# Softmax attention: the low parts of the third expert weight on GpSimd in two operations

## The chip, the cores and the metric

The kernel runs on one core of a Trainium2 chip. The metric is the time of one execution on the device in microseconds (us), as the median of several executions; lower is better. The engines are TensorE (PE), VectorE (DVE), ScalarE (ACT), GpSimd (POOL) and SyncE (SP, which only issues DMAs here). Each runs its own queue of instructions in order, and they wait for each other by semaphores.

## What is computed

A decoder of two layers over x of 32 samples x 128 positions x 256 features: softmax attention, retention over a context, a mixture of eight experts, then three further stages. This case lies in the first stage. Its arithmetic per sample, with n the layer norm of x:

```
q = softmax(n Wq + bq, over the 256 features)
k = softmax(n Wk + bk, over the 128 positions)
v = softmax(n Wv + bv, over the 128 positions)
x = x + q (k^T v) / sqrt(256)
```

Beside it the first stage prepares data of later stages: the three expert weights W1, W2, W3 (each 128 x 8192 f32 in the kernel's layout) are multiplied by 256 and split into a high part in f16 and a low part in f16 (the value minus the high part), and both go to DRAM, where the expert stage reads them. The context is split in the same way, without a factor.

## The kernel before

The stage (softmax_attention) works in eight groups g of four samples (GB = 4, NG = 8). Each engine has one loop over j that takes, in an order written out by hand, steps of group j (projection of v and k), group j + 1 (statistics and normalisation) and group j - 1 (q, the product, the addition). PSUM is four areas pA to pD. I call a pass from one L483 to the next a round.

The weights' pieces: each weight w = 0, 1, 2 is cut into eight pieces n of 128x1024, one for each round, in two buffers each. SP loads piece n into pf[w][n % 2] (L347); ScalarE writes the high part to ph (L639, piece j in its pass j); VectorE writes the low part to pl by one scalar_tensor_tensor, pf x 256 - ph (L540, piece j - 1 in its pass j); SP waits for piece_low[w], stores both parts (L353) and loads piece n + 2, for w = 0, 1, 2 in turn.

VectorE's order in a pass: the addition to X (L534), statistics of the next group (L82 to L97), the shift of k (L496, L499), the reciprocal of v's sum (L504), the low part of the rows (L483), the largest of q (L514) and its shift (L516), the sum of k (L508, L510), the maximum of v (L489) and its shift (L496, L499), the low part of weight 1 (L540), qT (L523), the low parts of weights 0 and 2 (L540), the normalisation of the next group (L478), the reciprocal of q's sum (L527), the maximum of k (L489). In pass 3 centre_v follows (L546, L548), in passes 4 to 8 the low part of a retention weight (L554). The shifts L496 and L499 read and write 128x8 tiles in SBUF, L516 a 128x4 tile.

GpSimd's order in a pass: the reciprocal root of the next group's variance (invert, L675), the normalisation of v's exponentials (norm_v, L681), the low part of the context (context_lower, L686), both for group j - 1.

TensorE's order: the turned rows (L393), q (L419, L421), v (L262), the turned v (L430), the turned q (L438, which waits for ScalarE's exponentials L618, which wait for L516), k (L262), the product of k and q (attend, L445, which waits for qT), and the weighing of v (weigh, L453, which waits for ScalarE's copy L631). VectorE's addition L534 waits for L453.

Of the kernel before, what the change touches and what calls it, by code (L numbers as in the profile page):

```python
# [9 lines left out]
ALU = mybir.AluOpType  # L10
# [42 lines left out]
def spread(ap, n):  # L53

    return ap.unsqueeze(2).broadcast_to((ap.shape[0], ap.shape[1], n))
# [219 lines left out]
def softmax_attention(nc, sems, X, ident, power, A, ahead):  # L275

    SCALE = 16.0
    HALVES_SCALE = 256.0
    FEATURES = DC * GB
    with ExitStack() as scope:  # L280
        c = Core(nc, scope, sems, "a_")
# [23 lines left out]
        def samples(ps):  # L305
            return ps[:, :, :].rearrange("p a (b t) -> p (a b) t", t=S)
# [10 lines left out]
        def on(g, *work):  # L317
            if 0 <= g < NG:
                for w in work:
                    w(g)  # L320
# [3 lines left out]
        pf = [[c.sb(f"pf{w}{i}", [P, WIDE]) for i in range(2)] for w in range(3)]  # L324
        ph, pl = ([[c.sb(f"{n}{w}{i}", [P, WIDE], f16) for i in range(2)] for w in range(3)] for n in ("ph", "pl"))
        piece_in, piece_out = ([[c.sem(f"{n}{w}{i}") for i in range(2)] for w in range(3)] for n in ("piece_in", "piece_out"))
        piece_high, piece_low = ([c.sem(f"{n}{w}") for w in range(3)] for n in ("piece_high", "piece_low"))

        cf, ctx16 = ([c.sb(f"ctx{i}", [P, DC * GT]) for i in range(2)],
                     [[c.sb(f"ctx16{t}{i}", [P, DC * GT], f16) for i in range(2)] for t in range(2)])  # L330
# [7 lines left out]
        with nc.Block() as block:  # L338
# [128 lines left out]
            def _(dve):  # L467
# [18 lines left out]
                def maximum(n, ps):  # L486
                    def work(g):
                        dve.wait_ge(s[n + "_projected"], g + 1)
                        dve.tensor_reduce(mx[n][:, :], samples(ps), AX, ALU.max).then_inc(s[n + "max"], 1)  # L489
                    return work  # L490

                def shift(n, at):
                    def work(g):
                        bias = spread(bkv[:, at, :], GB)
                        dve.wait_ge(s[n + "max"], g + 1)
                        dve.scalar_tensor_tensor(by_chunk(mb[n]), by_chunk(mx[n]), 1.0 / SCALE, bias, ALU.mult, ALU.add)\  # L496
                           .then_inc(s[n + "maxb"], 1)
                        dve.wait_ge(s[n + "maxb"], g + 1)
                        dve.tensor_tensor(by_chunk(nb[n]), bias, by_chunk(mb[n]), ALU.subtract).then_inc(s[n + "shift"], 1)  # L499
                    return work  # L500
# [36 lines left out]
                def piece_lower(w):  # L537
                    def work(n):
                        dve.wait_ge(piece_high[w], n + 1)
                        dve.scalar_tensor_tensor(pl[w][n % 2][:, :], pf[w][n % 2][:, :], HALVES_SCALE, ph[w][n % 2][:, :],  # L540
                                                 ALU.mult, ALU.subtract).then_inc(piece_low[w], 1)
                    return work

                def centre_v():
                    dve.wait_ge(later_in, 16 * len(RETENTION))
                    dve.tensor_reduce(wsum[:, :], by_head, AX, ALU.add).then_inc(v_summed, 1)  # L546
                    dve.wait_ge(v_summed, 1)
                    dve.scalar_tensor_tensor(by_head, spread(wsum[:, :], HD), -1.0 / HD, by_head, ALU.mult, ALU.add)\  # L548
                       .then_inc(v_centred, 1)

                def later_lower(i):
                    n = RETENTION[i]
                    dve.wait_ge(later_high, i + 1)
                    dve.scalar_tensor_tensor(flat(R[n][1]), later[n], HALVES_SCALE, flat(R[n][0]), ALU.mult, ALU.subtract)\  # L554
                       .then_inc(later_low, 1)
# [14 lines left out]
                for j in range(NG + 2):  # L570
                    on(j - 2, add)
                    on(j + 1, stats)
                    on(j - 1, shift("k", 0))
                    on(j + 1, lambda g: rs.combine(dve, g))
                    on(j - 1, invert_v)
                    on(j, rows_low)
                    on(j - 1, shift_q, invert_k)
                    on(j, maximum("v", pD), shift("v", 1))
                    on(j - 1, piece_lower(1), take_q, piece_lower(0), piece_lower(2))
                    on(j + 1, norm)  # L580
                    on(j - 1, invert_q)
                    on(j, maximum("k", pC))
                    if j == 3:
                        centre_v()
                    if 0 <= j - 4 < len(RETENTION):
                        later_lower(j - 4)
# [84 lines left out]
            @block.gpsimd  # L671
            def _(pool):
                def invert(g):
                    pool.wait_ge(rs.ve_done, g + 1)
                    pool.tensor_tensor(rstd[:, :], rs.ve[:, :], power[:, 0:GB], ALU.pow).then_inc(s["rstd"], 1)  # L675

                def norm_v(g):
                    pool.wait_ge(s["vrec"], g + 1)
                    if g > 0:
                        pool.wait_ge(s["vn_turned"], g)  # L680
                    pool.tensor_tensor(samples(vn), samples(ex["v"]), spread(rec["v"][:, :], S), ALU.mult)\  # L681
                        .then_inc(s["vn"], 1)

                def context_lower(g):
                    pool.wait_ge(ctx_high, g + 1)
                    pool.tensor_tensor(ctx16[1][g % 2][:, :], cf[g % 2][:, :], ctx16[0][g % 2][:, :], ALU.subtract)\  # L686
                        .then_inc(ctx_low, 1)

                invert(0)
                for j in range(NG + 1):  # L690
                    on(j + 1, invert)
                    on(j - 1, norm_v, context_lower)


def starts(value, n):
# [2857 lines left out]
def decoder(nc, A, out, stages):  # L3553
    with ExitStack() as whole:
        c = Core(nc, whole, [], "")
        X = c.sb("X", [P, B, D])
        ident = c.sb("ident", [P, P])
        power = c.sb("power", [P, 64])
        work = {"softmax_attention": softmax_attention, "retention": retention, "moe_swiglu": moe_swiglu,
                "lie": lie_rotation, "mqa": one_key_attention, "moe_silu": moe_silu}  # L3560
        sems = []
# [124 lines left out]
```

## Time and profile before

| | us |
|---|---|
| median of 3 runs | 1486.89 |
| lowest and highest | 1485.07, 1488.93 |
| the profiled execution | 1483.58 |
| its span in the trace | 1481.8 |

The span is the time from the first to the last instruction in the trace; 1.8 us of the profiled execution lie around it. Times in the rows are counted from the start of the span. "Busy" is the time in which an engine has an instruction in work. Of TensorE the profile also gives the granted clock, as a share of 2.4 GHz: 1.00 or 0.50. The first stage takes the first 172 us of the span.

### The profile page before, as it was taken

To read this page: it belongs to the slowest core of one execution; us is meant where nothing else is said; L and a number is where in the kernel's file an instruction comes from. 1 tells how busy PE (TensorE), PEld (TensorE's weight loads), DVE (VectorE), ACT (ScalarE), POOL (GpSimd) and SP (SyncE) were. 2 spreads that over 40 slices of the span, in tenths; PEclk is the share of its full clock that TensorE was granted. 3 is DMA by queue.
4 is the path that set the end of the run, shared out by engine and by line. 5 is a ranking of instruction groups with operands and counts; after the bars stand their busy time and mean duration, and the time that the engine had idled before them with its cause. 6 is when DMAs were issued, how large, how long until landed. Compare 5 with 4: busy or idle time off the path is not lost. (4 is left out here: it accounts for less than half of the span.)

```text
span 1481.8 us, 29874 instructions
## 1 busy us (share of the span) xinstructions
PE 1209.2 (82%) x10673; PEld 871.6 (59%) x10673; DVE 1007.5 (68%) x2053; ACT 723.0 (49%) x1388; POOL 462.4 (31%) x437
## 2 busy tenths in 40 slices
PE   4999579989766379999999914992799976999997
PEld 2656356777545369999999902931445532665564
DVE  5999567887665846666666557575778785667653
ACT  4778455555324134444444414043356656756643
POOL 1322164564322044545455311156344211000000
PEclk9999789999996589999999965555899997999999
DMA  7666358567603722222332163001745403033131
GB/s 283 228 243 230 134 97 154 102 125 104 80 2 149 309 81 92 94 94 93 97 101 82 49 240 138 2 1 39 178 68 101 86 3 115 15 129 131 28 129 29
DMA packets 99977, 165.03 MB, mean 111 GB/s; under 512 B 14902, under 2 KB 63738, under 8 KB 98556
## 3 DMA queue, kind: packets, MB, share of 16 engines
q1 hardware_dynamic: 91964, 142.40, 34.2%
q0 software_dynamic: 7488, 20.46, 4.5%
q8 instruction: 92, 1.51, 0.4%
q14 instruction: 49, 0.40, 0.1%
q10 hardware_dynamic: 384, 0.26, 0.1%
HBM read 110.61 MB, written 52.30 MB: 110 GB/s over the span
## 5 line engine op out<-in xcount | busy, mean ns | idle before, releaser
L1075 POOL DMA_INDIRECT expert_results<-mt_yout,m_deliver x78 | 77.2, 990 | 149.2 <-ACT mt_yout L1163 137.2
L1108 PE MATMUL mt_pU<-mt_xh,m_w 128*128 128x256 f16 x624 | 116.2, 274 | 1.5 <-DVE mt_xl L1193 1.5
L1534 DVE TENSOR_TENSOR r_sim<-r_pS,r_causal 128x512 f32<-128x512 f32 x128 | 86.5, 683 | 43.8 <-PE r_pS L1444 43.0
L1108 PE MATMUL mt_pV<-mt_xh,m_w 128*128 128x256 f16 x624 | 115.4, 273 | 0.0
L1067 POOL DMA_INDIRECT mt_xin<-token_rows,m_fetch x78 | 86.7, 1111 | 81.4 <-POOLq L782 57.9
L2958 ACT ACTIVATE q_ex<-q_pE 128x512 f32<-128x512 f32 x128 | 75.1, 601 | 74.1 <-PE q_pE L2590 73.4
L1119 PE MATMUL mt_pY<-m_w,mt_hh 128*128 x624 | 106.4, 273 | 1.0 <-DVE mt_hl L1207 1.0
L1157 ACT ACTIVATE mt_hh<-ahead 128x512 f16<-128x512 f32 x78 | 49.2, 631 | 118.7 <-DVE ahead L1202 118.7
L3262 PE MATMUL s_pY<-s_w,s_hh 128*128 128x256 f16 x576 | 99.9, 273 | 8.0 <-DVE s_hl L3482 6.3
L2687 DVE TENSOR_REDUCE q_mx<-q_pS 128x4 f32<-128x512 f32 x128 | 85.4, 684 | 29.7 <-PE q_pS L2569 29.2
L1199 DVE TENSOR_TENSOR ahead<-mt_pU,ahead 128x512 f32<-128x512 f32 x78 | 54.0, 692 | 57.7 <-ACT ahead L1151 57.7
L1207 DVE TENSOR_TENSOR mt_hl<-ahead,mt_hh 128x512 f16<-128x512 f32 x78 | 54.0, 692 | 54.3 <-ACT mt_hh L1157 54.3
L3334 ACT ACTIVATE s_h<-s_pU,s_b 128x512 f32<-128x512 f32 x72 | 49.4, 687 | 81.5 <-PE s_pU L3248 81.3
L3475 DVE TENSOR_TENSOR s_hc<-s_h,s_spread_share 128x512 f32<-128x512 f32 x64 | 44.2, 691 | 65.2 <-ACT s_h L3334 65.2
L1108 PE MATMUL mt_pU<-mt_xl,m_w 128*128 128x256 f16 x312 | 85.6, 274 | 0.0
L1108 PE MATMUL mt_pV<-mt_xl,m_w 128*128 128x256 f16 x312 | 85.2, 273 | 0.0
L1119 PE MATMUL mt_pY<-m_w,mt_hl 128*128 x312 | 85.0, 273 | 0.0
L1151 ACT ACTIVATE ahead<-mt_pU 128x512 f32<-128x512 f32 x78 | 46.6, 597 | 65.8 <-PE mt_pU L1108 65.8
L3262 PE MATMUL s_pY<-s_w,s_hl 128*128 128x256 f16 x288 | 78.5, 273 | 0.0
L3248 PE MATMUL s_pU<-s_XH,s_w 128*128 128x512 f16 x216 | 73.1, 379 | 0.0
L3262 PEld LDWEIGHTS s_pY<-s_w,s_hh 128*128 128x128 f16 x576 | 52.3, 98 | 31.7 <-DVE s_hl L3482 15.0
L1108 PEld LDWEIGHTS mt_pU<-mt_xh,m_w 128*128 x624 | 61.4, 98 | 8.9 <-issue 1.9
(593 smaller groups left out, 3458.7 us busy)
## 6 DMA issues: line engine op xcount, KB each, us to landing
s_spread_share<-shares SPq DMA_DIRECT2D x32, 512.0 KB, 6.1
a_pf<-in_L_ffn_W SPq DMA_DIRECT2D x24, 512.0 KB, 6.4
m_w<-split_w SPq DMA_DIRECT2D x6, 2048.0 KB, 19.0
split_w<-a_ph SPq DMA_DIRECT2D x24, 256.0 KB, 3.8
split_w<-a_pl SPq DMA_DIRECT2D x24, 256.0 KB, 4.2
r_kstack<-k_bounce SPq DMA_DIRECT2D x48, 128.0 KB, 3.9
r_qstack<-q_bounce SPq DMA_DIRECT2D x48, 128.0 KB, 5.7
q_Q<-m_bounce SPq DMA_DIRECT2D x24, 256.0 KB, 7.5
```

Source lines behind the costliest of these rows:

```text
L1067: pool.indirect_dma_start(xin[n % INPUTS][:, a, :], None, rows[:, :], bass.IndirectOffsetOnAxis(ap=fetch[:, at:at + 1], axis=0))\
L1075: pool.indirect_dma_start(results[:, :], bass.IndirectOffsetOnAxis(ap=deliver[:, at:at + 1], axis=0), yout[n % 2][:, a, :], None).then_inc ...
L1108: last = pe.matmul(ps[half][:, j, :], W[x][:, e, dc, cols], (xh, xl)[y][p][:, dc, :], start=(m == 0), stop=(m == len(steps) - 1))
L1119: last = pe.matmul(pY[:, a, :], (hh, hl)[x][half][:, j, a * P:(a + 1) * P], W3[y][:, e, half * HALF + j, :], start=half == 0 and j == 0 an ...
L1199: dve.tensor_tensor(t_[half][:, :, :], pU[half][:, :, :], sg[half][:, :, :], ALU.mult).then_inc(t_done, 1)
L1207: dve.tensor_tensor(hl[half][:, :, :], h[half][:, :, :], hh[half][:, :, :], ALU.subtract)\
L1534: dve.tensor_tensor(sim[n % SIMS][:, :].rearrange("p (h t) -> p h t", t=S), pS[n % 2][:, :].rearrange("p (h t) -> p h t", t=S), repeat(tab ...
L2687: dve.tensor_reduce(mx[:, at:at + UNIT], pS[n % 2][:, :, :], AX, ALU.max).then_inc(s["taken"], 1)
L2958: act.activation(ex[n % RING][:, :], pE[n % 2][:, :], ACT.Exp, scale=ATT).then_inc(s["exp"], 1)
L3248: last = pe.matmul(pU[k % RING][:, :], W1[x][:, j, dc, :], rows_of(("XH", "XL")[y], g * GT, (g + 1) * GT)[:, dc, :], start=(n == 0), stop= ...
L3262: last = pe.matmul(pY[:, b, :], (hh, hl)[x][k % RING][:, b * S:(b + 1) * S], W2[y][:, j, :], start=(j == 0 and n == 0 and b % 2 == 0), sto ...
L3334: act.activation(h[k % RING][:, :], pU[k % RING][:, :], ACT.Silu, bias=b1[:, k % N:k % N + 1], scale=1.0 / SCALE).then_inc(h_done, 1)
```

## The change

The low part of the third weight (w = 2) leaves VectorE's pass, and GpSimd makes it after the context's low part. GpSimd does it in two operations: it multiplies pf by 256 in place (tensor_scalar, 128x1024 f32 to f32), waits for that on a new semaphore piece_scaled, and subtracts ph (tensor_tensor, 128x1024, f32 and f16 to f16). Both read and write SBUF. The stores and loads of SP wait for the same semaphore piece_low[2] as before.

```diff
--- before.py
+++ after.py
@@ -325,6 +325,7 @@
         piece_high, piece_low = ([c.sem(f"{n}{w}") for w in range(3)] for n in ("piece_high", "piece_low"))
+        piece_scaled = c.sem("piece_scaled")
@@ -576,7 +577,7 @@
                     on(j, maximum("v", pD), shift("v", 1))
-                    on(j - 1, piece_lower(1), take_q, piece_lower(0), piece_lower(2))
+                    on(j - 1, piece_lower(1), take_q, piece_lower(0))
                     on(j + 1, norm)
@@ -686,10 +687,18 @@
+                def piece_lower(n):
+                    pool.wait_ge(piece_high[2], n + 1)
+                    pool.tensor_scalar(pf[2][n % 2][:, :], pf[2][n % 2][:, :], HALVES_SCALE, None, ALU.mult)\
+                        .then_inc(piece_scaled, 1)
+                    pool.wait_ge(piece_scaled, n + 1)
+                    pool.tensor_tensor(pl[2][n % 2][:, :], pf[2][n % 2][:, :], ph[2][n % 2][:, :], ALU.subtract)\
+                        .then_inc(piece_low[2], 1)
+
                 invert(0)
                 for j in range(NG + 1):
                     on(j + 1, invert)
-                    on(j - 1, norm_v, context_lower)
+                    on(j - 1, norm_v, context_lower, piece_lower)
```

## Rows read from the trace of the kernel before

**Rows 1.** The page, part 1: busy time and share of the span.

```profile
PE 1209.2 (82%) x10673; PEld 871.6 (59%) x10673; DVE 1007.5 (68%) x2053; ACT 723.0 (49%) x1388; POOL 462.4 (31%) x437
```

**Rows 2.** Busy by window: length, busy us of each engine, clock, DMA share, GB/s.

```profile
50.93:68.22 17.29, 16.04 (x101) 10.69 (x100) 16.62 (x37) 13.33 (x40) 4.96 (x3) 1.00 0.69 235
68.22:86.32 18.10, 16.03 (x101) 10.68 (x100) 17.83 (x40) 13.84 (x42) 4.97 (x3) 1.00 0.72 254
```

**Rows 3.** Timeline of VectorE, round from 103.70: start, duration, instruction, [idle before].

```profile
106.04 0.61 DVE L516 TENSOR_SCALAR a_nqshift<-a_nqmax 128x4 f32<-128x4 f32 x1
...
109.12 0.17 DVE L496 SCALAR_TENSOR_TENSOR a_vmaxb<-a_vmax,a_bkv 128x8 f32<-128x8 f32 x1
109.32 0.17 DVE L499 TENSOR_TENSOR a_vshift<-a_bkv,a_vmaxb 128x8 f32<-128x8 f32 x1
109.41 1.22 DVE L540 SCALAR_TENSOR_TENSOR a_pl<-a_pf,a_ph 128x1024 f16<-128x1024 f32 x1
110.54 1.22 DVE L523 TENSOR_TENSOR a_qT<-a_pA,a_krec 128x1024 f32<-128x1024 f32 x1
111.68 2.35 DVE L540 SCALAR_TENSOR_TENSOR a_pl<-a_pf,a_ph 128x1024 f16<-128x1024 f32 x2
...
117.03 1.66 DVE L534 SCALAR_TENSOR_TENSOR X<-a_pB,a_rq,X 128x256 f32<-128x256 f32 x4
```

**Rows 4.** Timeline of TensorE in the same round.

```profile
112.28 1.95 PE L445 MATMUL a_pB<-a_qT,a_kexp 128*128 128x128 f32 x16
114.92 1.99 PE L453 MATMUL a_pB<-a_vt,a_aT 128*128 128x256 f32 x8 [0.69 <-ACT a_aT L631]
```

**Rows 5.** Timelines: the addition in two earlier rounds, the weighing before the second.

```profile
64.18 1.66 DVE L534 SCALAR_TENSOR_TENSOR X<-a_pB,a_rq,X 128x256 f32<-128x256 f32 x4 [0.43 <-PE a_pB L453]
...
79.45 1.99 PE L453 MATMUL a_pB<-a_vt,a_aT 128*128 128x256 f32 x8 [0.69 <-ACT a_aT L631]
...
82.28 1.65 DVE L534 SCALAR_TENSOR_TENSOR X<-a_pB,a_rq,X 128x256 f32<-128x256 f32 x4
```

**Rows 6.** Timeline of GpSimd in the round from 103.70.

```profile
104.73 1.89 POOL L681 TENSOR_TENSOR a_vn<-a_vexp,a_vrec 128x1024 f32<-128x1024 f32 x1
106.58 2.13 POOL L686 TENSOR_TENSOR a_ctx<-a_ctx 128x1024 f16<-128x1024 f32 x1
```

**Rows 7.** Two lines' instructions on GpSimd in a later stage: duration ns min/median/max.

```profile
L3039 POOL COPY q_KM<-q_K x8: 602/602/604, 1034.9 to 1179.4; 48x512 f16<-48x512 f16 x8
...
L3030 POOL TENSOR_SCALAR q_xn<-X,q_rs_mean,q_rstd x32: 1209/1220/1267, 1018.3 to 1154.7; 128x256 f32<-128x256 f32 x32
```

**Rows 8.** Three lines on VectorE, durations as before; then two timeline rows.

```profile
L2234 DVE SCALAR_TENSOR_TENSOR l_R<-l_R,l_rr,ahead x32: 472/474/2581, 974.9 to 1008.9; 128x256 f32<-128x256 f32 x32
...
L516 DVE TENSOR_SCALAR a_nqshift<-a_nqmax x8: 170/607/616, 36.3 to 157.3; 128x4 f32<-128x4 f32 x8
...
L514 DVE TENSOR_REDUCE a_nqmax<-a_pB x8: 1214/1216/1225, 35.1 to 156.1; 128x4 f32<-128x1024 f32 x8
...
204.89 2.13 POOL L1752 TENSOR_TENSOR r_ksplit<-r_kturned,r_ksplit 128x1024 f16<-128x1024 f32 x1
...
205.08 1.96 DVE L88 TENSOR_TENSOR r_rs_apart<-r_rs_stat 128x4 f32<-128x4 f32 x1
```

**Rows 9.** Timelines of GpSimd and VectorE in the last round.

```profile
155.13 2.13 POOL L686 TENSOR_TENSOR a_ctx<-a_ctx 128x1024 f16<-128x1024 f32 x1
...
157.34 0.17 DVE L516 TENSOR_SCALAR a_nqshift<-a_nqmax 128x4 f32<-128x4 f32 x1
```

**Rows 10.** Timeline of TensorE behind gaps; a window behind the second (clock 0.50).

```profile
161.94 3.78 PE L445 MATMUL a_pB<-a_qT,a_kexp 128*128 128x128 f32 x16 [1.32 <-DVE a_qT L523]
...
375.33 0.44 PE L270 MATMUL r_pB<-r_wV,r_ch 128*128 128x256 f16 x2 [2.27 <-DVE r_crossed L1523]
...
375.60:378.90 3.30, 3.30 (x29) 2.43 (x29) 0.97 (x3) 0.00 (x0) 3.22 (x4) 0.50 1.12 104
...
431.20 0.28 PE L1486 MATMUL r_pB<-r_bias_rows,r_ones 128*128 128x256 f16 x1 [2.17 <-DVE r_gl L1552]
```

## The prediction

> **What bounds the kernel now.** The change touches the first stage only, about 170 of the 1481.8 us of the span, so I read that stage. In the busy shares TensorE leads over the whole span, 82% against 68% for VectorE [rows 1]; that is an average over six stages and says little here. Cut into rounds (one round works on one group of four samples), a round is 17.29 to 18.10 us, and VectorE is busy for 16.62 to 17.83 us of it, TensorE for about 16.0 [rows 2]. So VectorE looks like the bound, with 0.2 to 0.7 us to spare. The timelines tell it more exactly. In the round that starts at 103.70 VectorE's queue runs without a wait and reaches the residual addition (L534) at 117.03 [rows 3]. That addition needs the weighing on TensorE (L453), which starts at 114.92, lasts 1.99 and ends at 116.91 [rows 4]. The two arrive 0.1 us apart. TensorE's path to it goes by the scores (L445, at 112.28), which need qT from VectorE (L523, 110.54 to 111.76, so 0.5 us of slack), then by a copy on ScalarE that costs the 0.69 us of wait in front of L453 [rows 4]. After the addition, statistics and small steps lead to the next round's L483, and again to both engines. Two chains of equal length, then: VectorE's whole queue, and VectorE's start of the round followed by TensorE. In the round before 68.22 VectorE already waits 0.43 us for the weighing; only the round with centre_v has VectorE arriving later, at 82.28, with no wait [rows 5].
>
> **What is removed.** The third low part on VectorE, eight instructions of L540. Two of them in a row take 2.35 us and one 1.22, so each occupies 1.13 us of the queue [rows 3]. It stands behind qT and before the rows' normalisation, that is on VectorE's chain alone. By itself the removal gains 0.06 us in a round such as this one (from 117.03 to just behind 116.91), nothing where VectorE waits already, and 0.8 us in the centre_v round (the weighing there ends at 81.44, the addition starts at 82.28 [rows 5]). The last two rounds gain nothing: VectorE waits there. Summed: 0.8 + 3 x 0.06 = 1.0 us, out of 9 us of VectorE work that leave.
>
> **What is added.** GpSimd gets, behind the context difference (L686, 106.58 to 108.71 [rows 6]), a scale of 128x1024 and a difference. Then it would be idle until its next reciprocal root some 12 us later, so its own queue has room: nothing waits behind the new pair. Its input, ScalarE's third high part, was made a round earlier. The difference has the very form of L686, two f32/f16 inputs to f16, so 2.13 us [rows 6]. The scale has no row in this stage. The nearest rows: a copy of 48x512 f16 takes 0.60, so 1024 elements 1.2 at most; a tensor_scalar of 128x256 f32 with two operations and two column operands takes 1.22, so 1024 elements up to 4.9 [rows 7]. I take 1.5, near the copy, since one operation with a constant is nearer to it; 1.1 and 4.9 stay as ends. The wait on piece_scaled costs the 0.1 us of one semaphore and has nothing behind it but the difference.
>
> **What the addition does to VectorE.** This is the term that decides. Rows of before show a VectorE instruction held back while GpSimd works. In the lie stage L2234, three SBUF inputs, 128x256, takes 472 ns at least and up to 2581. L88, 128x4, a size that takes 0.17 in L499, takes 1.96 us; it starts at 205.08 and ends at 207.04, and GpSimd's L1752 runs from 204.89 to 207.02 [rows 8]. In this stage itself L516, a tensor_scalar of 128x4, takes 607 ns in the median and 170 at least [rows 8]; in the round shown it ends at 106.65, and GpSimd's L681 at 106.62 [rows 3, 6]. Instructions with a PSUM input are not held: L514, which reads PSUM and runs beside L681 in most rounds, lasts 1214 to 1225 ns in all eight [rows 8]. So the instructions with all inputs in SBUF stand still until GpSimd's one has ended. The Trainium skill, "SBUF — State Buffer", section "Who interferes with whom", gives this as a lock on a shared port pair, taken by a VectorE instruction with two SBUF inputs or by a GpSimd one that reads SBUF, whichever is first, for its whole length; it speaks against this change, and the trace agrees: L2234 is held for up to 2.1 us, 2581 ns in place of 472 [rows 8]. With it the sum is the one below, without it the 1.0 us of gain above.
>
> Before, GpSimd is done at 108.71 and VectorE's SBUF-only steps begin at 109.12 (L496), 109.32 (L499) and 109.41 (L540) [rows 3]: just free of each other. With the change the scale runs from 108.67 to 110.17. L496, issued at 109.12, ends at 110.20. The difference starts at about 110.26; L499 would start within 0.03 us of it. Either L499 is held or it slips through and L540 behind it is held; in both cases the next large step starts at about 112.4, when the difference ends. L540 then runs, and qT starts 1.13 later at 113.5 instead of 110.54: 3.0 later. Its slack of 0.5 is used up and the scores start 2.5 later, at 114.8, the weighing ends at 119.4. VectorE, 3.0 late and 1.13 shorter, arrives at 118.9 and waits. The addition comes 2.45 late: the round's price. Next in the line are the loads of the next pieces, which SP issues behind L540's second step: up to 3.0 later, while ScalarE's reading of them moves by 2.45 as well, so I cost them at nothing.
>
> Five rounds have this shape (L681 at 34.5, 52, 87, 104.7, 122): 5 x 2.45 = 12.25. The centre_v round is VectorE's: 3.0 - 1.13 = 1.85. In the last two rounds L516 comes after the context difference. In the last the scale would run from 157.22 to 158.72, and L516, issued at 157.34 and done at 157.51, ends at 158.75: 1.25 late, with ScalarE's exponentials and the scores behind it [rows 9]; the one before has the same shape. That is 2.5. Sum: 12.25 + 1.85 + 2.5 = 16.6 us. Every 0.1 us of the scale is in each of the eight rounds, so 1.1 would give 13.4 and 4.9 would give 43.8. The Trainium skill, "GPSIMD Engine Reference", section "Engine selection", has one-input work at roughly line rate, some 0.9 us for 1024 elements at its 1.2 GHz as an estimate; the sum would then be about 12, and no row here shows it for a scale.
>
> **TensorE's clock.** TensorE now gets a gap of 2.5 us in front of the scores in each of six rounds, with the 0.69 behind it. In the trace of before a gap of 2.27 us is followed by 3.3 us at a granted 0.50, that is 1.2 instead of 2.4 GHz; one of 2.17 us is not [rows 10]. Five gaps of TensorE between 1.6 and 2.6 us start at the high level in the first 450 us, these two among them, and four are followed by the low one. The scores take 3.78 us at the low level, 1.95 at the high [rows 4, 10]. A low stretch of 3.4 us that holds the 0.7 us wait loses half of the other 2.7: 1.4 us. Six rounds x 0.8 x 1.4 = 6.7; bounds are none, 0, and 6 x 1.83 = 11. I take 6.7, since the rows speak for four in five.
>
> **The forecast.** 16.6 + 6.7 = 23.3 us on the profiled execution of 1483.6, so 1506.9. That execution lies 3.3 under the median of 1486.9; on the median the forecast is 1510.2.
>
> **Rivals.** (1) L540 goes ahead of the difference. L499 slips through, L540 follows at 110.3, before GpSimd's instruction has its turn, and the difference runs beside qT, which is not held. The scores come 0.45 late, the second L540 is held for a microsecond, and the addition comes 0.6 late. Six rounds x 0.6 + 2.5 = 6.1, so 1493.0. For it: the two start within 0.03 us. Against it: L540 would be 0.05 behind the difference by my count. (2) The other side, not slower: large SBUF-only instructions are not held by these two, and only the removal counts, 1.0 us less, 1485.9. It decides in each round at 109.12, where L496 would have to end while the scale runs. Against it stand all of rows 8. (3) The scale is slow, 3.5 us between the ends: 16.6 + 8 x 2.0 + 8 for the clock = 40.6, so 1527.5.
>
> **Chances.** The forecast 0.65, (1) 0.15, (2) 0.08, (3) 0.12. A measurement of this kernel tells about 0.3% from no change, 4.5 us. Slower by more holds the forecast, (3) and nearly all of (1): 0.87. The same is (2) and the small end of (1): 0.11. Faster by more would need four times the gain of (2): 0.02. The range from 1493 to 1528 leaves out (2) and a part of (1) below and scales over 3.5 us above, less than 0.2.
>
> **What would show it.** Of the changed kernel I expect rounds of about 20 us, L496 at about 1 us, L499 or the first L540 at over 2 us, L516 in the last two rounds at 1.4, a wait of 2.5 us of L445 for L523, and a granted clock of 0.5 now and then from 40 to 140 us. If L496 and L540 keep 0.17 and 1.22 us, (2) holds. If the first L540 is short and the second long, it is (1). The duration of the scale's row sizes everything; if it is over 3 us, the time is over 1520.

## The result and the profile after

| | median us | lowest, highest | 
|---|---|---|
| before, 20 runs | 1485.54 | 1483.41, 1490.75 |
| after, 20 runs | 1489.55 | 1485.30, 1496.44 |

The ratio of after to before is 1.0026, with a 95% interval of 1.0016 to 1.0037: the change costs 4 us. The sign was forecast, the size was not: 1510.2 was the forecast, with a range from 1493 to 1528, and its rise of 23.3 us is nearly six times the one measured.

The same round as in [rows 3], of the changed kernel. First GpSimd, then VectorE, from their timelines (start us, duration us, engine, line, instruction):

```profile
107.43 2.13 POOL L687 TENSOR_TENSOR a_ctx<-a_ctx 128x1024 f16<-128x1024 f32 x1
109.53 2.78 POOL L692 TENSOR_SCALAR a_pf<-a_pf 128x1024 f32<-128x1024 f32 x1
112.39 2.14 POOL L695 TENSOR_TENSOR a_pl<-a_pf,a_ph 128x1024 f16<-128x1024 f32 x1
```

```profile
109.98 0.61 DVE L497 SCALAR_TENSOR_TENSOR a_vmaxb<-a_vmax,a_bkv 128x8 f32<-128x8 f32 x1
110.62 0.17 DVE L500 TENSOR_TENSOR a_vshift<-a_bkv,a_vmaxb 128x8 f32<-128x8 f32 x1
110.71 1.22 DVE L541 SCALAR_TENSOR_TENSOR a_pl<-a_pf,a_ph 128x1024 f16<-128x1024 f32 x1
111.84 1.22 DVE L524 TENSOR_TENSOR a_qT<-a_pA,a_krec 128x1024 f32<-128x1024 f32 x1
112.98 2.64 DVE L541 SCALAR_TENSOR_TENSOR a_pl<-a_pf,a_ph 128x1024 f16<-128x1024 f32 x1
115.54 1.37 DVE L479 TENSOR_SCALAR a_xn<-X,a_rs_mean,a_rstd 128x256 f32<-128x256 f32 x4
```

The scale (L692) takes 2.78 us. L497, which was 0.17 us before, is held and ends at 110.59, that is 1.06 us after the scale's start and 1.7 us before its end. L500 and the first low part then run at their old lengths beside the rest of the scale; qT, which reads PSUM, follows at its old length. Only the second low part meets the difference (L695): issued at 112.98, it ends at 115.62, 1.09 us behind the difference's end at 114.53, so it is held 1.42 us.

TensorE in that round. The scores start 0.05 us behind qT's end (0.52 before) and show no wait for it; the weighing has its old wait; what has grown is the wait for the addition, from 0.18 us before to 0.83:

```profile
113.11 2.05 PE L446 MATMUL a_pB<-a_qT,a_kexp 128*128 128x128 f32 x16
115.85 1.99 PE L454 MATMUL a_pB<-a_vt,a_aT 128*128 128x256 f32 x8 [0.69 <-ACT a_aT L632]
119.55 0.28 PE L420 MATMUL a_pB<-a_bias_rows,a_ones 33*128 33x256 f16 x1 [0.83 <-DVE X L535]
```

Busy by window, one row a round (length, then busy us of PE, weight load, DVE, ACT, POOL, clock). The first is the round with centre_v, 18.86 us against 18.10 before; the second is the round above, 18.14 us against 17.38 before:

```profile
67.52:86.38 18.86, 16.11 (x101) 10.61 (x100) 18.59 (x38) 13.81 (x41) 9.88 (x5) 1.00 0.71 248
104.52:122.66 18.14, 16.12 (x101) 10.61 (x100) 17.90 (x38) 13.81 (x42) 9.89 (x5) 1.00 0.67 235
```

The last two rounds: L517 (L516 before) is held there, and in the last but one L497 meets the difference. Three lines with their durations in ns (min, median, max), then from the timelines that round's L497, and the scale and L517 of the last round:

```profile
L541 DVE SCALAR_TENSOR_TENSOR a_pl<-a_pf,a_ph x16: 1174/1218/2641, 38.6 to 167.2; 128x1024 f16<-128x1024 f32 x16
...
L517 DVE TENSOR_SCALAR a_nqshift<-a_nqmax x8: 169/644/950, 35.3 to 161.3; 128x4 f32<-128x4 f32 x8
...
L497 DVE SCALAR_TENSOR_TENSOR a_vmaxb<-a_vmax,a_bkv x8: 167/612/1473, 27.3 to 146.4; 128x8 f32<-128x8 f32 x8
...
146.37 1.47 DVE L497 SCALAR_TENSOR_TENSOR a_vmaxb<-a_vmax,a_bkv 128x8 f32<-128x8 f32 x1
...
161.21 2.77 POOL L692 TENSOR_SCALAR a_pf<-a_pf 128x1024 f32<-128x1024 f32 x1
...
161.32 0.95 DVE L517 TENSOR_SCALAR a_nqshift<-a_nqmax 128x4 f32<-128x4 f32 x1
```

L517, a tensor_scalar, is also let go 1.06 us behind the scale's start, long before the scale's end at 163.98.

A good measure of the stage is the time from the start of GpSimd's first L681 to the start of its last (L682 in the changed kernel), seven rounds. In the two kernels that were traced twice it repeats to within 0.03 us, while their medians differ by 3.4 and 3.7 us from one session to the other (below).

```profile
34.54 1.90 POOL L681 TENSOR_TENSOR a_vn<-a_vexp,a_vrec 128x1024 f32<-128x1024 f32 x1
...
153.28 1.90 POOL L681 TENSOR_TENSOR a_vn<-a_vexp,a_vrec 128x1024 f32<-128x1024 f32 x1 [12.77 <-DVE a_vrec L504]
```

```profile
33.47 1.90 POOL L682 TENSOR_TENSOR a_vn<-a_vexp,a_vrec 128x1024 f32<-128x1024 f32 x1
...
157.26 1.90 POOL L682 TENSOR_TENSOR a_vn<-a_vexp,a_vrec 128x1024 f32<-128x1024 f32 x1 [9.44 <-DVE a_vrec L505]
```

Before it is 118.7 us, after 123.8: 5.05 us more. By round, before and after: 17.4 and 17.6, 17.3 and 17.6, 18.1 and 18.9 (centre_v), 17.4 and 18.1, 17.4 and 18.1, 14.4 and 15.2, 16.7 and 18.4. The next stage's first VectorE instruction starts at 173.24 before and at 176.88 after, only 3.6 us later, for two reasons. TensorE's 128x512 matmuls of the first round shorten from 0.63 to 0.38 us at about 24.7 in the changed kernel's trace and at about 27.4 in that of before, and the first L682 comes 1.1 us earlier (the granted clock reads 1.00 on both sides of that change, so its cause is not shown). And the last weighing took 1.99 us at a granted clock of 1.00, where before it took 3.78 at 0.50. Neither is shown to come from the edit; in the second trace of the changed kernel, below, the last addition starts 6.5 us later than before.

### The profile page after: what moved, and what is told of

Same layout as the page of the kernel before. It is cut to its first block and busy times, and to the rows that moved or that the text cites. A ratio compares the mean times of both kernels' runs of the same rounds, so it can differ in the third digit from the quotient of the medians.

```text
span 1489.4 us, 29882 instructions
## 1 busy us (share of the span) xinstructions
PE 1210.2 (81%) x10673; PEld 871.0 (58%) x10673; DVE 1011.9 (68%) x2045; ACT 722.7 (49%) x1388; POOL 502.3 (34%) x453
```

## The experiments

Each ratio stands against the kernel before on the same chip. "Seven rounds" is the measure above, 118.7 us before and 123.8 after; it is of one trace each. The diffs are extracts, with ... for what is left out: those of the single parts are taken against the changed kernel, the fills and the copy against the removal alone, and those under "The pair in other places" each against the version that it is built on. What a kernel leaves out of the computation stands in its expectation.

### The removal alone

```diff
-                    on(j - 1, norm_v, context_lower, piece_lower)
+                    on(j - 1, norm_v, context_lower)
...
-                    sp.wait_ge(piece_low[w], n + 1)
+                    sp.wait_ge((piece_low[0], piece_low[1], piece_high[2])[w], n + 1)
```

> The removal alone: the third weight's low part is made by nobody, VectorE's instruction is gone, GpSimd's two are gone too; zeros, set once, are stored in its place, so that part of the output's arithmetic is left out. Measure: from the start of the first to the start of the last normalisation of v on GpSimd (L681 before, L682 after), seven rounds, 118.7 us before and 123.8 us after. Theory A (VectorE's queue and TensorE's chain are within 0.1 us of each other, only the round with centre_v has 0.8 us in it): 117.7 us, the total 1.0 us under before. Rival (VectorE is the bound through the whole stage): 1.1 us in each round, 111 us, the total 8 us under before.

Seven rounds: 117.5 us. Ratio 0.9994, interval 0.9983 to 1.0006. The first five rounds are all 17.3 us, that with centre_v too; the last two keep their lengths. So 9 us of work taken off VectorE are worth 1.2 us of the stage: theory A's size, not the rival's. TensorE's chain stood right behind VectorE's queue.

### The addition alone

```diff
-                    on(j - 1, piece_lower(1), take_q, piece_lower(0))
+                    on(j - 1, piece_lower(1), take_q, piece_lower(0), piece_lower(2))
...
+                    pool.tensor_scalar(spare[:, :], spare[:, :], 1.0, None, ALU.mult).then_inc(piece_scaled, 1)
+                    pool.wait_ge(piece_scaled, n + 1)
+                    pool.tensor_tensor(spare_out[:, :], spare[:, :], spare_high[:, :], ALU.subtract).then_inc(spare_low, 1)
```

> The addition alone: VectorE keeps its three low parts as before, and GpSimd makes a scale and a difference of the same shapes and types on tiles of their own (ones), at the same place. Theory A (the difference holds VectorE's next SBUF-only instruction to its end, 1.4 us a round, the scale holds it for 1.06 us from its start, 0.4 us a round, and VectorE's queue has no room): 1.4 to 1.9 us a round, 130.5 us in the seven rounds, the total 13 us over before, near 1499. Rival B (most of the 4 us between before and after comes from the stages behind, not from GpSimd's two operations): under 122 us in the seven rounds and the total within 5 us of before.

Seven rounds: 133.1 us. Ratio 1.0091, interval 1.0072 to 1.0110, the median 14.3 us over before. GpSimd's two instructions on tiles that nobody else touches cost this, so what costs is their place beside VectorE, not a dependence. Of the 133.1, some 2.5 us are put down to TensorE's clock: one round took 21.8 us, the next 19.3. There TensorE waited 2.21 us for the addition, and the window behind the wait has the granted clock at 0.50 (TensorE's timeline, then the windows):

```profile
87.20 0.39 PE L421 MATMUL a_pB<-a_bias_rows,a_ones 33*128 33x256 f16 x1 [2.21 <-DVE X L536]
...
87.10:93.70 6.60, 6.50 (x27) 3.37 (x28) 4.27 (x18) 2.17 (x8) 3.35 (x3) 0.50 0.65 256
93.90:100.00 6.10, 5.24 (x34) 3.21 (x32) 5.80 (x6) 3.60 (x10) 6.02 (x3) 1.00 0.50 172
```

### The difference alone, and the scale alone

```diff
-                    pool.tensor_scalar(pf[2][n % 2][:, :], pf[2][n % 2][:, :], HALVES_SCALE, None, ALU.mult)\
-                        .then_inc(piece_scaled, 1)
-                    pool.wait_ge(piece_scaled, n + 1)
```

> After without the scale: GpSimd makes the difference alone, right behind the context's; the multiplication by 256 of the third weight before its low part is left out. Theory A (a difference holds to its end): it now starts at about 108.7 of a round like that from 103.70, holds the first small shift for 1.6 us, qT is 1.5 late with 0.5 of slack, the scores start 1.2 late: 125.5 to 127 us in the seven rounds, total 9 to 10 us over before, that is more than with the scale in front. Rival C (the price is the scale's, 2.8 us long): without it the seven rounds take 118 us, and the total is that of before.

Seven rounds: 126.3 us. Ratio 1.0048, interval 1.0032 to 1.0064, the median 8.3 us over before. Against the changed kernel the seven rounds are 2.5 us longer; its medians, 4.0 and 7.7 us over before in two sessions, are too far apart to say the same. Taking 2.8 us of GpSimd's work away made the stage slower. GpSimd, VectorE and TensorE in the round from 108.09 of this run:

```profile
113.06 2.14 POOL L692 TENSOR_TENSOR a_pl<-a_pf,a_ph 128x1024 f16<-128x1024 f32 x1
...
113.52 1.70 DVE L497 SCALAR_TENSOR_TENSOR a_vmaxb<-a_vmax,a_bkv 128x8 f32<-128x8 f32 x1
115.26 0.17 DVE L500 TENSOR_TENSOR a_vshift<-a_bkv,a_vmaxb 128x8 f32<-128x8 f32 x1
...
117.75 2.05 PE L446 MATMUL a_pB<-a_qT,a_kexp 128*128 128x128 f32 x16 [0.91 <-DVE a_qT L524]
```

The difference runs 113.06 to 115.20 and L497 ends at 115.22: held to the difference's end. And now the hold lies ahead of qT, so the scores wait for it: the shape of the forecast's round, with a rise of 1.1 us.

```diff
-                    pool.wait_ge(piece_scaled, n + 1)
-                    pool.tensor_tensor(pl[2][n % 2][:, :], pf[2][n % 2][:, :], ph[2][n % 2][:, :], ALU.subtract)\
-                        .then_inc(piece_low[2], 1)
```

> After without the difference: GpSimd makes the scale alone; the third weight's low part is left out and zeros stored. Theory A (a scale of 2.8 us holds VectorE for 1.06 us only, and that is hidden by the instruction that left): 118.5 us in the seven rounds, 0.8 us of hold on the shift of q in each of the last two, total 0 to 1 us over before. Rival C (the scale holds for all of its 2.8 us): the first small shift is held for 2.2 us, the scores come 1.8 late, 129 us in the seven rounds and the total 12 us over before.

Seven rounds: 118.9 us. Ratio 0.9998, interval 0.9988 to 1.0008. The hold by the scale is the same 0.44 us of L497 (and 0.78 us of the shift of q in the last two rounds), and the leaving of VectorE's third low part pays for it. So the difference's hold of the second low part makes the change slow, not the longer scale; the late difference, below, shows the same with the whole computed.

### What holds what: a write alone, and a copy

```diff
+                def spare_work(n):
+                    for i in range(2):
+                        if n + i > 0:
+                            pool.wait_ge(spare_low, 2 * n + i)
+                        pool.memset(spare[:, :], 0.0).then_inc(spare_low, 1)
```

> As the removal alone (the third low part left out, zeros stored), and GpSimd fills a spare 128x1024 f32 tile with zeros twice, some 1 us each, where the scale stood; it reads nothing. Theory A (what holds VectorE is GpSimd's reading of SBUF): the first small shift keeps 0.17 us and the low part 1.22, seven rounds 117.6 us. Rival E (any GpSimd instruction on SBUF holds VectorE's SBUF-only ones): the first small shift at 0.6 us or more and the next ones too, 118.5 us or more.

Seven rounds: 118.1 us. The fills lie over L500 (L497 of the changed kernel) and do not hold it; but they do hold the shift of q (L520, 0.83 us in the last two rounds). GpSimd's and VectorE's timelines, then two lines' durations:

```profile
107.93 1.95 POOL L698 MEMSET a_spare<- 128x1024 f32 x2
...
108.40 0.17 DVE L500 SCALAR_TENSOR_TENSOR a_vmaxb<-a_vmax,a_bkv 128x8 f32<-128x8 f32 x1
...
L500 DVE SCALAR_TENSOR_TENSOR a_vmaxb<-a_vmax,a_bkv x8: 166/166/167, 28.5 to 142.3; 128x8 f32<-128x8 f32 x8
...
L520 DVE TENSOR_SCALAR a_nqshift<-a_nqmax x8: 210/610/831, 36.5 to 156.9; 128x4 f32<-128x4 f32 x8
```

Both theories were half right. L500, with two SBUF inputs, is held by GpSimd instructions that read SBUF and not by one that only writes it; the tensor_scalar L520, with one SBUF input, is held by that one too. This kernel and the next ran once, so only their traces count.

```diff
+                    pool.tensor_copy(spare_to[:, :], spare[:, :]).then_inc(spare_low, 1)
```

> As the removal alone, and GpSimd copies a spare 128x1024 f32 tile to another where the scale stood. Theory A (a one-input GpSimd instruction reads its 1024 columns in about 1 us and holds VectorE only so long; the rest of the scale's 2.8 us is arithmetic and writing): the copy lasts 1.0 to 1.3 us and the first small shift 0.6, the same as beside the scale. Rival F (the hold is a share of the instruction's length, 1.06 of 2.78): the small shift is held for 0.4 us less and lasts 0.17 to 0.2.

Seven rounds: 118.6 us. The copy takes 1.04 us and holds as long as the scale does:

```profile
107.34 1.04 POOL L696 COPY a_spare_to<-a_spare 128x1024 f32<-128x1024 f32 x1
...
107.81 0.60 DVE L500 SCALAR_TENSOR_TENSOR a_vmaxb<-a_vmax,a_bkv 128x8 f32<-128x8 f32 x1
```

L500 ends 1.07 us after the copy's start; beside the scale it was 1.06. Rival F is out: the hold is not a share of the length. It fits a scale that reads its 1024 columns in about 1 us and then computes and writes for 1.7 more; the inner working is argued from the lengths of the holds, not seen.

### The pair in other places

All of these compute the whole. The difference late, behind the maximum of k:

```diff
+                    if n + 1 < NG:
+                        pool.wait_ge(s["kmax"], n + 2)
                     pool.wait_ge(piece_scaled, n + 1)
```

> The whole computation. After, with the difference on GpSimd waiting until VectorE has made the maximum of k of the next group (at the end of VectorE's pass), so that it runs beside the addition, which reads PSUM. Theory A (the difference's hold of VectorE's second low part, 1.4 us, is what makes after slow): the hold is gone, VectorE is early by 0.7 us and waits for TensorE, rounds of 17.4 us, 118.9 us in the seven rounds as with the scale alone, total 0 to 1 us over before. Rival D (the hold only moves, to the retention weight's low part and the small steps of the statistics behind the addition): over 120.5 us in the seven rounds, total 3 us over before.

Seven rounds: 120.3 us. Ratio 1.0013, interval 0.9997 to 1.0029. All rounds but one are as with the scale alone (17.4); the centre_v round is 18.9, as in the changed kernel, since its second instruction (L549, both inputs in SBUF) now meets the difference. In one round of seven, rival D was right; its total of 3 us over before did not come. Then the scale late too:

```diff
                     pool.wait_ge(piece_high[2], n + 1)
+                    pool.wait_ge(piece_low[1], n + 1)
```

> The whole computation. As the run before, and the scale waits until VectorE has made the low part of the second weight, so that its first microsecond lies beside qT, which reads PSUM. Theory A: no hold of the first small shift (0.17 us instead of 0.61) and none of the shift of q in the last two rounds (0.17 instead of 0.95): 117.6 us in the seven rounds, total 1.0 us under before, that is the gain of the removal alone. Rival D: the scale's hold falls on the first weight's low part or the normalisation and the difference's on the steps behind the addition: over 119 us in the seven rounds.

Seven rounds: 119.3 us. Ratio 0.9983, interval 0.9970 to 0.9997. Rounds of 17.3 and again 18.9 with centre_v; rival D has the sum (over 119), but by this one round. GpSimd's and VectorE's timelines of that round and of one without, the held instructions last:

```profile
80.01 2.14 POOL L698 TENSOR_TENSOR a_pl<-a_pf,a_ph 128x1024 f16<-128x1024 f32 x1 [2.39 <-DVE a_kmax L490]
...
80.55 2.15 DVE L549 SCALAR_TENSOR_TENSOR ahead<-a_wsum,ahead 128x512 f32<-128x512 f32 x1
...
111.05 2.78 POOL L693 TENSOR_SCALAR a_pf<-a_pf 128x1024 f32<-128x1024 f32 x1 [2.07 <-DVE a_pl L541]
...
111.94 1.23 DVE L541 SCALAR_TENSOR_TENSOR a_pl<-a_pf,a_ph 128x1024 f16<-128x1024 f32 x1
113.08 1.84 DVE L479 TENSOR_SCALAR a_xn<-X,a_rs_mean,a_rstd 128x256 f32<-128x256 f32 x4
```

The scale's first microsecond lies beside qT. Its tail (to 113.83) leaves the low part alone and holds the normalisation's tensor_scalar until about its end: the four take 1.84 us instead of 1.37, and all of it falls on the first, issued 2.0 us behind the scale's start (0.88 us instead of 0.40). So a tensor_scalar can be held in the scale's tail, while L517 of the changed kernel, issued 0.1 us behind the scale's start, was let go after 1.06; the scale's hold of such instructions is not one piece. VectorE has the room for it there. The hold goes the other way too: in the rounds with a retention weight, L555 (both inputs in SBUF, 116.06 to 116.73) is first, and the difference issued at 116.21 takes 2.51 us instead of 2.14. On another chip the same kernel came out otherwise:

> The run with both late once more, beside the one above on one chip. Theory A: 119.3 us in the seven rounds, total 1 to 2.5 us under before. Rival (its first total, 2.5 us under before, was noise): total at before or over it.

Seven rounds: 119.3 us again, but ratio 1.0012, interval 0.9995 to 1.0028. The two medians, 1484.1 and 1487.8, are of one kernel; so is the pair of the changed kernel below. The kernel before had medians from 1485.3 to 1485.8 in all five sessions. An interval of one such session does not hold all the scatter of a variant, and no total here supports a claim of less than about 3 us. The difference beside the addition instead:

```diff
-                        pool.wait_ge(s["kmax"], n + 2)
+                        pool.wait_ge(s["x_done"], GB * n + 1)
```

> The whole computation. As the run with both late, but the difference waits for the first row of VectorE's addition of the same group instead of the maximum of k, so that it runs beside the rest of the addition and the statistics, and centre_v's second instruction is no longer held (it cost 1.5 us in its one round). Theory A: every round 17.3 us, 117.6 us in the seven rounds against 119.3 with both late, total 1 to 3 us under before, not over the run with both late. Rival G (the store and the next load of the third weight's piece now go out 3 us later and ScalarE waits for the load): rounds over 18 us, waits of ScalarE for the third piece, total at before or over it.

Seven rounds: 119.4 us. Ratio 1.0004, interval 0.9991 to 1.0017. The centre_v round falls to 17.5 as expected, but the last two of the seven rise by 1.0 and 0.6, where no statistics of a next group stand between the addition and the small steps, and L497 (the shift of k) takes 1.14 us instead of 0.15. Rival G was wrong: ScalarE has no wait for a piece. (Nor has it in the changed kernel.) In the one pass only:

```diff
-                    if n + 1 < NG:
+                    if n == 2:
+                        pool.wait_ge(s["x_done"], GB * n + 1)
+                    elif n + 1 < NG:
                         pool.wait_ge(s["kmax"], n + 2)
```

> The whole computation. As the run with both late, but in the one pass with centre_v the difference waits for the addition's first row instead of the maximum of k. Theory A: the 1.5 us that the difference cost there are gone and the last rounds stay as with both late: 117.8 us in the seven rounds against 119.3, total 1.5 us under the run with both late and 2 to 4 us under before. Rival H (what the stage gains is given back behind it): seven rounds as said, total as before.

Seven rounds: 117.9 us, 0.9 us under before and 5.9 under the changed kernel. Ratio 0.9987, interval 0.9974 to 1.0001: the best whole version by the stage, and by the total not told from before. Whether the gain of the stage is lost behind it (rival H) the totals can't tell.

### The changed kernel again

> The changed kernel itself once more, beside the one above on one chip. Theory A: 3 to 5 us over before, 123.8 us in the seven rounds, the same holds as in its first trace (L497 0.61, the second L541 2.64, L517 0.95 in the last two). Rival B (the slowdown was a matter of the chip or of the clock's phase): within 1.5 us of before.

Seven rounds: 123.8 us, with the same holds. Ratio 1.0046, interval 1.0031 to 1.0060. The slowdown repeats; it is 4.0 and 7.7 us by the medians, and by the stage 5.05 and 5.03.

## Why the prediction was wrong

- **Two chains of equal length.** Right. The removal alone gave 1.2 us in the seven rounds against 1.0 forecast, and the first five rounds came to TensorE's 17.3.
- **GpSimd holds VectorE's SBUF-only instructions.** Right for those that decide here, and so the sign; by the prediction's own bound for a telling difference, 4.5 us, the first comparison (4.0) would still pass as the same and only the second (7.7) as slower. L497 and L517 are held where it was expected, a low part too (the second in the place of the first), and the addition alone cost 14 us. The lock that the Trainium skill gives in "SBUF — State Buffer", section "Who interferes with whom", also has the exception that a write alone does not hold an instruction with two SBUF inputs; the fills bear it out with 0.17 us. That the lock is kept "for the whole instruction" does not hold for the scale here: 1.06 of 2.78 us. As the prediction put it, "the instructions with all inputs in SBUF stand still", it is too wide. The sum of k, a tensor_reduce of one SBUF tile, runs beside L686 already in the kernel before (106.58 to 108.71), and both keep their lengths, 1.21 and 2.13 us; and with the difference beside the addition, the statistics L82, which read one SBUF tile, keep theirs (1.39 us for four) beside it:

```profile
106.56 1.21 DVE L508 TENSOR_REDUCE a_ksum<-a_kexp 128x8 f32<-128x1024 f32 x1
...
116.19 2.13 POOL L698 TENSOR_TENSOR a_pl<-a_pf,a_ph 128x1024 f16<-128x1024 f32 x1 [3.92 <-DVE X L535]
...
117.20 1.39 DVE L82 BATCH_NORM_STATS2 a_rs_stat<-X 128x6 f32<-128x256 f32 x4
```

- **The scale's length: 1.5 us taken, 2.78 measured.** Wrong as a size, within the ends of 1.1 and 4.9. But by my rule of 0.8 us for each 0.1 us it would have made the time 10 us longer, and it did not, since the next step is the one that failed. (The line-rate estimate of 0.9 us beside it fits GpSimd's copy, 1.04 us, and not the scale.)
- **The step that failed: "L496, issued at 109.12, ends at 110.20", with the scale's end.** I let an instruction hold VectorE for its whole duration because the rows of before that I went by all had a two-input instruction on GpSimd. The scale holds for 1.06 us. This leaves 1.8 us between the end of the hold and the start of the difference, and in it L500 and the first low part get through, with qT, which nothing holds, behind them. The forecast had qT 3.0 us late; counted from the start of L681 (L682) in its round it is 0.45 late, which uses up the 0.5 of slack, and the scores show no wait. In its place the difference falls on the second low part, 1.42 us, which TensorE's path does not need. With the measured sizes the round is 0.44 + 1.42 - 1.13 = 0.73 us longer; it was 0.76. (The first two rounds rose by only 0.14 and 0.27, since VectorE had waited there before.) The scale's longer tail is what protects qT: with the scale left out, the forecast's mechanism appears, and the rise is 1.1 us a round.
- **Rival (1) had the order right** ("the second L540 is held for a microsecond"), though by another cause than the one it gave; its rise of 6.1 us is the nearest of the four to the 4.0 measured.
- **The last two rounds: 2.5 us.** Right in kind, wrong in size: L517 was held 0.78 us in each instead of 1.25, and the seventh round rose by 1.64: to that hold comes L497, which there met the difference for 1.3 us and left the scores waiting 0.77 us for qT, and that was not forecast.
- **The clock: 6.7 us.** Not there: the granted clock is 1.00 from 33 to 155 us of the changed kernel's trace. The term hung on the 2.5 us wait of the scores, which did not come. Where a wait of 2.21 us did come, in the addition alone, the low clock followed.
- **The range.** Its upper end varied the scale; its lower end was the time of rival (1), the one other shape of the round that was priced, and the measured time lies 3.5 us under it. The shape was the uncertain part, and no shape was priced in which the hold ends before GpSimd's instruction does.

What stays open: between the profiled executions the span rose by 7.6 us, 3.6 of it by the end of the first stage and the rest behind it, 3.2 of it in the last but one stage. That stage lasts 229.1 to 232.6 us over all traces, 229.3 in the one of before and 232.5 and 232.4 in the two of the changed kernel; runs with like edits lie at both ends. Whether the edit has a part in it was not followed up.

## What to carry to other kernels

Before work goes from VectorE to GpSimd, lay both timelines over each other and ask, for each VectorE instruction that would run beside the new one, where its inputs lie. Here those with two SBUF inputs wait for a GpSimd instruction that reads SBUF, and a tensor_scalar from SBUF to SBUF waits even for one that only writes; those that read PSUM do not, nor do a tensor_reduce and the statistics of one SBUF tile. The price depends less on how long GpSimd's instruction is than on which instruction it meets, and on whether the critical chain needs that one. Here the same two instructions cost 5 us or gain 1 of the stage by the two waits that place them.

## What was not expected of the hardware

- GpSimd's tensor_scalar by a constant, 128x1024 f32 in place, takes 2.78 us, its copy of the same size 1.04, and the two-input difference to f16 2.14.
- The tensor_scalar holds VectorE's two-input instructions for 1.06 us from its start, as long as the copy does. A VectorE tensor_scalar with one SBUF tile as input is let go at 1.06 us when it comes 0.1 us behind the start (L517, 128x4), and held to about the end when it comes 2.0 us behind it (L479, 128x256, with both late). What happens between, and whether the size has a part in it, no run here shows.
- The difference holds to its end: L497 ends at 115.22 and the difference at 115.20 in the run with the difference alone.
- Two fills with zeros (0.98 us each) hold a VectorE tensor_scalar (0.83 us instead of 0.17), and a scalar_tensor_tensor with two SBUF inputs not at all.
